# A graph layer on one core: message steps of six and five groups, and three gather groups fetched row by row from another queue

## The reference, cut to what matters

```python
xn = layernorm(x)
# graph layer: mean over the incoming edges of a node, then two linear maps
summed = segment_sum(xn[src], dst, N)
agg = summed / max(counts, 1)
gnn = relu(agg @ W_l.T + b_l + xn @ W_r.T) + xn
# linear attention over all nodes, then an MLP ("message")
Q, K = elu(xn @ Wq) + 1, elu(xn @ Wk) + 1
KV = einsum('nshd,nshv->nhdv', K, (xn @ Wv) / N)
msg = layernorm(attention(Q, KV) @ Wm) * g1 + b1
h = relu(concat[xn, msg] @ W1) @ W2
mix = xn + layernorm(h) * g2 + b2
x = x + gnn + mix
# then a feed-forward on the half of the nodes that a learned score picks
x = x + ffn(layernorm(x))
```

## Time and profile before

| | |
|---|---|
| time, median of 3 runs | 2594.31 us (2593.91 to 2596.81) |
| the profiled execution | 2591.4 us, its span 2589.7 us |
| PE, POOL, DVE, ACT busy | 2200.0, 1696.3, 1316.4, 902.0 us |
| mean granted TensorE clock | 0.937 of full speed |
| gathers (L713) | 1563, 949 ns each |

### The profile page before, as it was taken

How to read it: one execution, slowest core, us unless ns; L and a number is a source line. 1 busy time by engine, 2 the same in 40 slices (tenths; PEclk the granted TensorE clock), 3 DMA queues, 4 the chain that set the end, 5 groups by cost and what they waited for, 6 DMA issues and landing times.

```text
span 2589.7 us, 48874 instructions
## 1 busy us (share of the span) xinstructions
PE 2200.0 (85%) x13352; PEld 1826.8 (71%) x13353; DVE 1316.4 (51%) x3156; ACT 902.0 (35%) x1949; POOL 1696.3 (66%) x1817
## 2 busy tenths in 40 slices
PE   1399999997888888888888888888999899589998
PEld 1287777775667667666676666767777678379998
DVE  8644444443444344454444445544555589844444
ACT  8433333331222222222222222222232258444554
POOL 3577777777777777777777777777777511045553
PEclk6699999998998999999999999999999999689999
DMA  9766666664555555555555555555555489711111
GB/s 332 231 194 187 183 185 180 187 179 149 153 162 156 154 154 165 153 162 156 154 154 152 159 159 162 156 154 154 158 169 158 147 258 295 264 34 46 45 43 35
DMA packets 218372, 419.29 MB, mean 162 GB/s; under 512 B 40579, under 2 KB 107141, under 8 KB 218286
## 3 DMA queue, kind: packets, MB, share of 16 engines
q0 software_dynamic: 88352, 243.57, 33.0%
q1 hardware_dynamic: 129118, 173.95, 20.0%
q10 hardware_dynamic: 816, 0.79, 0.1%
HBM read 321.63 MB, written 96.52 MB: 161 GB/s over the span
## 4 chain that ended last, share of the span: by engine, by line
POOL 37%; PE 37%; issue 14%; DVE 5%; DMA 4%; ACT 1%; DVEq 1%; POOLq 0%; SPq 0%; ACTq 0%
POOL gath_raw L713 37%; PE ps L1779 11%; PE ps L1626 4%; PE ps L1547 3%; PE ps L1719 3%; PE ps L1549 3%; PE ps L1592 3%; DMA gath_raw<-xtab,srcI 3%; PE ps L1636 2%; PE ps L1532 2%; DVE stats L791 1%; PE ps L1674 1%; PE ps L1644 1%; DVE gath_raw L810 1%; PE ps L1715 1%
## 5 line engine op out<-in xcount | busy, mean ns | idle before, releaser
L713 POOL DMA_INDIRECT gath_raw<-xtab,srcI x1563 | 1484.0, 949 | 476.5 <-issue 464.0
L1547 PE MATMUL ps<-gath_raw,onehot 128*128 128x256 f16 x1956 | 477.4, 282 | 205.0 <-DMA gath_raw<-xtab,srcI 115.5
L887 DVE SCALAR_TENSOR_TENSOR onehot<-ps,blkbase,dstF 128x512 f32 x489 | 354.0, 745 | 255.3 <-issue 170.8
L1549 PE MATMUL ps<-gath_raw,onehot 128*128 128x257 f16 x1956 | 478.4, 282 | 0.0
L1547 PEld LDWEIGHTS ps<-gath_raw,onehot 128*128 x1956 | 194.7, 100 | 290.3 <-issue 260.6
L1626 PE MATMUL ps<-work,w_s 128*128 128x256 f32 x1568 | 394.6, 408 | 2.5 <-issue 1.7
L1626 PEld LDWEIGHTS ps<-work,w_s 128*128 128x128 f32 x1568 | 312.5, 205 | 49.8 <-issue 2.7
L961 DVE BATCH_NORM_STATS2 stats<-ps 128x6 f32<-128x256 f32 x196 | 74.4, 422 | 456.7 <-PE ps L1674 452.1
L1779 PE MATMUL ps<-split_raw 128*128 128x256 f32 x2376 | 293.0, 285 | 1.7 <-DVE split_raw L1226 1.5
L1779 PEld LDWEIGHTS ps<-split_raw 128*128 128x128 f32 x2376 | 288.1, 193 | 2.4 <-issue 1.9
L1360 ACT ACTIVATE work<-ps 128x512 f32<-128x512 f32 x98 | 58.5, 597 | 499.5 <-PE ps L1626 499.5
(11 more groups left out here) (215 smaller groups left out, 2990.5 us busy)
## 6 DMA issues: line engine op xcount, KB each, us to landing
work<-x_in SPq DMA_DIRECT2D x98, 256.0 KB
lin_raw<-lin_d POOLq DMA_DIRECT2D x49, 512.0 KB, 4.6
gath_raw<-xtab,srcI POOLq DMA_INDIRECT x1563
agg<-x_in SPq DMA_DIRECT2D x14, 896.0 KB, 7.9
xt_d<-work SPq DMA_DIRECT2D x49, 256.0 KB, 4.3
q_d<-work SPq DMA_DIRECT2D x49, 256.0 KB, 2.5
work<-q_d SPq DMA_DIRECT2D x49, 256.0 KB, 3.3
work<-xt_d SPq DMA_DIRECT2D x49, 256.0 KB, 3.1
```

The source lines that it names most:

```text
L713: e.indirect_dma_start(out=gath[:, TPG * s + t, 0:2 * D], out_offset=None, in_=xtab[:, :], in_offset=bass.IndirectOffsetOnAxis(ap=srcI[:, ...
L887: v.scalar_tensor_tensor(out=onehots[:, ds(p % OHN * TPG, TPG), :], in0=ps[:, columns:columns + 1, 0:P].to_broadcast(shape), scalar=blkbas ...
L1547: t.matmul(ps[:, ds(BG + k % 2, 1), 0:D], oh, gath[:, r, 0:D], start=False, stop=False, skip_group_check=True)
L1549: last = t.matmul(ps[:, ds(BG + k % 2, 1), 0:AGW], oh, gath[:, r, D:2 * D + 1], start=False, stop=q == TPG - 1, skip_group_check=True)
```

## The change

- **Steps.** The message steps take six and five groups in turn (`MPAIR`), 270 in all. 24 groups come behind the steps instead of seven. All steps are now in the loop; only the first two and the last are written out.
- **Place in the ring.** Two steps take eleven groups and the ring has six places, so a group's place changes from one pass of the loop to the next. PE computes it, `(m_first(s, j) + t) % RING`, and each matmul of a message step's `seg` takes the address of its rows from a register. Five semaphores are added (`rows_m`), so that the waits stay fixed to a position among the eleven. The groups behind the steps have constant places again.
- **Three groups row by row.** Groups 371 to 373 (`ROWG`) are not gathered by POOL. SP copies their 1536 rows of 1 KB with one DMA each, 32 in each of 48 message steps, into a buffer of their own (`rowt`). It loads 64 source numbers at a time (`row_list`) into the front of `bnd`, and takes 16 at a time into registers. The buffer has room for eight tiles beside `srcI`; the last four tiles go into the part of `srcI` whose groups are done, for which SP waits once, and then a column of ones is copied in.
- **Room.** The scratch for dynamic DMAs is halved, to 8192 bytes.
- **The end of the sums.** DVE adds the last two blocks' sums with one `add_before` ahead of the wait for the last group and one plain addition behind it, instead of two `add_before` behind it.
- Some semaphores are merged (`edges_set`, `bnd_moved`, `x_rows_in`, `s_placed`); DVE's key-step loop is one pass shorter, with three steps more written out.

```diff
-KG, MG = 2, 6
-NG = NSUP * (KG + MG)
+KG = 2
+MPAIR = (6, 5)
+NG = NSUP * 8
 RING = 6
-TAIL = 7
-MFULL = NSUP - TAIL
+MAT = KG * NSUP
+TAILAT = MAT + sum(MPAIR[i % 2] for i in range(NSUP))
+TAIL = NG - TAILAT
+ROWG = range(TAILAT + 3, TAILAT + 6)
+ROWT = len(ROWG) * TPG
+ROWB = 16
+ROWFREE = 8
...
+            def row_list(tile, half):
+
+                o = ROWG[0] * GE + tile * P + half * 4 * ROWB
+                of = src[o:o + 4 * ROWB] if isinstance(o, int) else src[ds(o, 4 * ROWB)]
+                e.dma_start(row_i, of.rearrange("(o e) -> o e", o=1)).then_inc(row_idx, 16)
+
+            def row_part(tile, half, part):
+
+                _, v = nc.values_load_multi_w_load_instructions(
+                    row_i[:, part * ROWB:(part + 1) * ROWB], engines=[mybir.EngineType.SP], min_val=0, max_val=NPAD - 1,
+                    skip_runtime_bounds_check_because="node numbers below the count of nodes")
+                for k in range(ROWB):
+                    p = half * 4 * ROWB + part * ROWB + k
+                    to = rowt[p:p + 1, ds(tile, 1) if not isinstance(tile, int) else slice(tile, tile + 1), 0:2 * D]
+                    e.dma_start(to.rearrange("p o c -> p (o c)"), xtab[ds(v[k], 1), :]).then_inc(by_row, 16)
+
+            def m_io(i, s, j, tile=None, half=0):
+                if tile is not None and s == 0:
+                    row_list(tile, half)
                 if not (isinstance(i, int) and i == NSUP - 1):
                     if past(i, 1):
                         e.wait_ge(m_xs, i)
                         e.wait_ge(m_nd_ps, i)
                     m_load(i + 1, 1 - s)
+                if tile is not None:
+                    if s == 0:
+                        e.wait_ge(row_idx, 16 * j + 16)
+                        alone(e, stood)
+                    row_part(tile, half, 2 * s)
                 if past(i, 2):
                     e.wait_ge(m_r, i - 1)
                     e.dma_start(turned(r_d, i - 2), flat(mr[s])).then_inc(r_out[s], 16)
...
                     m_load_xT(i + 1, 1 - s)
+                if tile is not None:
+                    row_part(tile, half, 2 * s + 1)
                 if past(i, 2):
                     l_store(i - 2, s)
...
             for g in range(NG):
+                if not fetched(g):
+                    continue
                 s = g % RING
...
-            def seg(slot, use, first, more, end):
-
-                padded = max(0, (use * RING + slot + 1) * TPG - (NG * TPG - GPAD)) if isinstance(use, int) else 0
-                landed = 16 * TPG * use + 16 * (TPG - min(TPG, padded))
+            def seg(rows_of, lists, slot, first, more, end, held=gath):
+
+                row = slot * TPG if isinstance(slot, int) else e.snap(slot * TPG)
+                landed_at = 16 * lists
                 with e.Fori(more, end + 1):
                     p, k = e.snap(pair), e.snap(full)
-                    e.wait_ge(rows_in[slot], landed)
+                    e.wait_ge(rows_of, landed_at)
...
                     for q in range(TPG):
                         oh = onehot[:, ds(p % OHN, 1), q, :]
-                        r = TPG * slot + q
-                        t.matmul(ps[:, ds(BG + k % 2, 1), 0:D], oh, gath[:, r, 0:D], start=False, stop=False,
+                        r = row + q if isinstance(row, int) else ds(row + q, 1)
+                        t.matmul(ps[:, ds(BG + k % 2, 1), 0:D], oh, held[:, r, 0:D], start=False, stop=False,
                                  skip_group_check=True)
-                        last = t.matmul(ps[:, ds(BG + k % 2, 1), 0:AGW], oh, gath[:, r, D:2 * D + 1], start=False,
+                        last = t.matmul(ps[:, ds(BG + k % 2, 1), 0:AGW], oh, held[:, r, D:2 * D + 1], start=False,
                                         stop=q == TPG - 1, skip_group_check=True)
...
+            def m_seg(s, j, t, span):
+
+                g = m_first(s, 0) + t
+                seg(landing(g), landed(g) + TPG * j, (m_first(s, j) + t) % RING, *span)
...
-            e.wait_ge(grp_used, NG)
-            add_before()
-            e.reg_mov(before, held)
-            e.reg_mov(since, pair)
-            add_before()
-            k = e.snap(full)
-            e.wait_ge(seg_added, k + 2)
+            add_before()
+            e.wait_ge(grp_used, NG)
+            b, k = e.snap(held), e.snap(full)
+            v.tensor_tensor(agg[:, ds(b, 1), :], agg[:, ds(b, 1), :], ps[:, ds(BG + k % 2, 1), 0:AGW], ALU.add).then_inc(sum_read, 1)
+            e.wait_ge(sum_read, k + 1)
...
-    nc = bacc.Bacc("TRN2", target_bir_lowering=False, num_devices=1)
+    nc = bacc.Bacc("TRN2", target_bir_lowering=False, num_devices=1, dynamic_dma_scratch_size=8192)
```

More of the change, by code:

```diff
@@ L276, in build @@
         rows_in = [sem(f"rows_in{i}") for i in range(RING)]
-        ones_set = sem("ones_set")
+        rows_m = [sem(f"rows_m{i}") for i in range(sum(MPAIR) - RING)]
+        row_idx = sem("row_idx")
+        by_row = sem("by_row")
         iota_ps = sem("iota_ps")
@@ L281, in build @@
         bnd_tab = sem("bnd_tab")
-        k_x_in = [sem(f"k_x_in{i}") for i in range(3)]
+        x_rows_in = [sem(f"x_rows_in{i}") for i in range(3)]
         k_xn = sem("k_xn")
@@ L299, in build @@
         kvbd_set = sem("kvbd_set")
-        m_x_in = [sem(f"m_x_in{i}") for i in range(2)]
         m_xT_in = [sem(f"m_xT_in{i}") for i in range(2)]
@@ L471, in seg_values, with m_first, fetched, landing @@
             return [tuple(v[3 * t:3 * t + 3]) for t in range(n)]
-        def k_place(s, j, t):
-            return KG * s + t, j
-        def m_first(i):
-            return KG * NSUP + MG * i - (max(0, i - MFULL) if isinstance(i, int) else 0)
-        def m_groups(i):
-            return MG - 1 if isinstance(i, int) and i >= MFULL else MG
-        def place(g):
-            return g % RING, g // RING
-        def m_place(i, t):
-            if isinstance(i, int):
-                return place(m_first(i) + t)
-            slot, use = place(KG * NSUP + t)
-            return slot, use + i
-        tail = list(range(NG - TAIL, NG))
+        def m_first(s, j):
+            return MAT + sum(MPAIR) * j + sum(MPAIR[:s])
+        def fetched(g):
+            return g not in ROWG
+        def landing(g):
+            p = (g - MAT) % sum(MPAIR)
+            return rows_m[p - RING] if MAT <= g < TAILAT and p >= RING else rows_in[g % RING]
+        def landed(g):
+            return TPG * len([o for o in range(g + 1) if landing(o) is landing(g) and fetched(o)])
         key_loads = [(wq_s[:, :, :], Wq.rearrange("(k p) n -> p k n", p=P)),
@@ L618, in m_io @@
                     m_load_xT(i + 1, 1 - s)
+                if tile is not None:
+                    row_part(tile, half, 2 * s + 1)
                 if past(i, 2):
                     l_store(i - 2, s)
-            steps(e, m_io, NSUP, 2)
+            e.wait_ge(grp_used, 2 * ROWB)
+            for s in range(2):
+                m_io(s, s, 0, 0, 0)
+            for tiles, half in ((range(ROWFREE), 0), (range(ROWFREE), 1), (range(ROWFREE, ROWT), 0), (range(ROWFREE, ROWT), 1)):
+                at = half * len(tiles) + 2 * ROWFREE * (tiles[0] // ROWFREE) - tiles[0]
+                if tiles[0] and not half:
+                    e.wait_ge(grp_used, (ROWT - ROWFREE) * RW // 2 // TPG + 1)
+                    with nc.allow_non_contiguous_dma("a column of ones"):
+                        e.dma_start(rowt[:, :, 2 * D:2 * D + 1], gath[:, 0:ROWT, 2 * D:2 * D + 1]).then_inc(by_row, 16)
+                with e.Fori(at + tiles[0] + (1 if at + tiles[0] == 0 else 0), at + tiles[-1] + 1) as j:
+                    for s in range(2):
+                        m_io(j * 2 + s, s, j, j - at, half)
+            m_io(NSUP - 1, (NSUP - 1) % 2, NSUP // 2)
             e.wait_ge(m_r, NSUP - 1)
@@ L1032, in m_body @@
                     l_even(i - 1, 1 - s, j - 1 + s)
-                for t in range(5, m_groups(i)):
+                for t in range(5, MPAIR[s]):
                     seg(g0 + t, BA, *spans[t])
-            steps(e, m_body, MFULL, 2)
-            for i in range(MFULL, NSUP):
-                m_body(i, i % 2, i // 2)
+            steps(e, m_body, NSUP, 2)
             last_two = [(i, own_m + 10 * NSUP - 10 + 5 * k) for k, i in enumerate((NSUP - 2, NSUP - 1))]
-            for t, g in enumerate(tail):
-                seg(g, BA, *seg_values(e, mybir.EngineType.DVE, g, 1)[0])
+            for t in range(RING):
+                seg(TAILAT + t, BA, *seg_values(e, mybir.EngineType.DVE, TAILAT + t, 1)[0])
                 if t in (0, 5):
@@ L1555, in seg @@
                 e.reg_alu(full, behind, 0, op=ALU.max)
[L1556 removed]
+                one = gath[:, 0, 2 * D:2 * D + 1]
                 k = e.snap(full)
@@ L1700, in _ @@
                     m_mlp_out(i)
+            with e.Fori(1, TAIL // RING - 1) as j:
+                spans = seg_values(e, mybir.EngineType.PE, TAILAT + RING * j, RING)
+                for k in range(RING):
```

(5 more changed lines are left out.)

118 lines of the change are left out of this document (60 added, 58 removed).

## The result

The changed kernel takes 2724.4 us (2721.5 to 2726.6) where the kernel before takes 2594.65: a ratio of 1.0502, 95% interval 1.0489 to 1.0514. It is slower by 5%; 2581 us was predicted.

A forecast was written before the change was run, and what follows sets the result against it. It took POOL's gathers to bound the kernel, with PE following. Gains of 15.0, 9.0 and 2.1 us (26.1) less 13 for register places gave -13.1 and 2581 us; the range was 2565 to 2618, the likeliest case 2572 to 2589.

The forecast's parts named there:

- The bound before: Message steps before the change: POOL's gathers set the time from 95 to 2054 us, 5.02 us a group; PE follows.
- Three groups less for POOL: POOL's gathers: 12 fewer at 1.254 us each, -15.0 us, if POOL still never waits.
- The tail: From the last gather's start to the last group's use: 9.3 us instead of 18.35, -9.0.
- DVE's end: The last additions of the sums: one addition and a wait stay of 2.68 us, -2.1.
- SP's rows at 0.5 us: SP's queue in the message steps: 32 rows take 16 us, fitting into its waits; cost 0, bound +60.
- Rival 3: SP's queue becomes the bound at 0.75 us a row or more: steps over 30 us, 2600 to 2650; chance 0.04.
- rest: Merged semaphores, DVE's three key steps written out, and a ones' column copied once: cost 0.
- The register places: PE's row addresses: eight more register instructions a pair at 0.10 us; after the ring POOL stops 12 us, rounded to +13.
- such a block: A block of 16 matmuls on PE, said to hide the register work of the first pair behind it.
- the last two stretches: Late message steps, at 1.37 and 1.41 pairs a group: PE's step forecast at 28.6 and 29.1 us.
- Rival 2: PE becomes the bound at 0.14 us a register instruction: +25 us, 2619, slower than before; chance 0.25.
- Scratch: Dynamic DMA scratch halved: three gathers under way are unaffected; cost 0, doubled waits +3.8 us.

The follow-up runs named there:

- e9b_static_no_rows: Changed kernel without SP's row DMAs, PE waiting for its own groups, PE's message steps written out twelve at a time with constant places: 2580.9 us.
- e10b: Changed kernel with SP's row destinations constant, PE waiting for its own groups, and PE's places constant: 2569.6 us, ratio 0.9893.
- e7: Changed kernel with SP's row destinations constant and PE waiting for its own groups, PE's places still in a register: 2640.4 us.
- e6: Changed kernel without SP's row DMAs (POOL gathers all groups) and with PE waiting for its own groups, places still in a register: 2632.4 us.
- e1_no_rows: Changed kernel without SP's row DMAs, POOL gathering all groups again, the rest kept: 2685.7 us, ratio 1.0332.
- e11: Changed kernel with PE's places constant and PE waiting for its own groups, SP's row destinations still in a register: 2740.0 us.
- e5: Changed kernel with only the semaphore choice altered, so that PE waits for its own groups: 2715.9 us, ratio 1.0464.
- e14b: e9b_static_no_rows with the place of the rows taken from a run-time counter in a register, steps still written out: 2644.5 us, ratio 1.0202.
- e8: e6 with the dynamic DMA scratch at its full size: 2632.45 us.

## Why the prediction was wrong, by its own steps

**The bound before.** Right: in e9b_static_no_rows and e10b POOL sets the pace again, and with PE's need above 27.6 us a step no gather that is taken away buys anything (e7 against e6).

**Three groups less for POOL, -15.0.** Measured -11.3 where POOL is the bound (e10b against e9b); in the profiled executions the last use comes 15.2 us earlier (2051.39 against 2066.61), and 3.1 us are lost in the stages behind, whose length varies between 512 and 518 us from one execution to another, so the term was right. Where PE or SP sets the steps it is worth next to nothing, which the prediction did not say: from the start of the last step to the last gather the changed kernel takes 118.1 us, and e1_no_rows with all gathers 120.2.

**The tail, -9.0, and DVE's end, -2.1.** Right, the first too small. From the last gather to the last use 6.27 us pass (2200.77 to 2207.04) where 18.35 did and 9.3 were predicted; from there to the sums 1.33 us in place of 3.73.

**SP's rows at 0.5 us, cost 0. This is the step that failed.** "With two addresses I take 0.5 us for a row (bounds 0.27 ... and 0.7 ...)": it takes 0.74, above the upper bound, so 32 rows are 23.7 us in place of 16, and SP is full. The bounds came from DMAs with a constant destination, and the added price was put on the address arithmetic. That is not where it lies: the register instruction and the move take 64 and 29 ns, the DMA itself 529 in place of 240, in one and the same kernel. Of 1536 rows 64 have a constant destination. The other 1472 account for (266626 - 222497)/1472 = 30 more DMA packets each than in e10b, and (89155 - 43524)/1472 = 31 more of under 512 B. The sizes of the packets in the trace say what they are: the changed kernel has 23,552 packets of 64 B, 16 for each of the 1472 rows, and e10b has none; in place of one packet of 1024 B a row there are 16 of 64 B and 15 more of 4 B. So a row of 1 KB with its destination in a register goes out in sixteen pieces. The Trainium skill (DMA: Bandwidth & Descriptors, section Why a DMA increments its semaphore by 16 and not by 1) says that software can split one contiguous run into a multiple of 16 so that the engines share it; the packets agree. SP's step became 31.1 us. From the start of the first step to that of the last the changed kernel takes 1485.2 us and e10b 1325.3, which is 159.9 us more; 3.7 come back by the last use, and the spans differ by 156.9 (2724.9 against 2568.0).

Rival 3 was the right mechanism with a chance of 0.04, and the measured 0.74 all but reached its threshold ("0.75 us a row or more"). Its time, 2600 to 2650, was too low, for a step of over 30 us was never multiplied out: 48 steps of 30.5 in place of 27.6 are 139 us more, less the 26 of gain, over 2700. Alone the rows cost 170 us (e11 against e10b); in the changed kernel taking them away bought 39, since two other costs stood behind them.

**The choice of semaphore, not priced.** The prediction's "rest" names merged semaphores at 0, and the text ahead of it says that the waits stay fixed to a position among the eleven; for PE's waits that is so, for the first six groups that POOL counts it is not. The new choice of a group's semaphore makes PE wait for up to the fifth group later: 38 us alone, 53 beside the register places, 8.5 behind SP's rows. Nothing of it can be read from the trace of before; it is in the diff, by writing down for pairs 1 to 5 which group completes the count that is waited for.

**The register places, +13.** The count was right: a pair has 17 register instructions in place of 9. The price of a step was too small: 47 to 71 us in all. "So a first pair behind such a block is free. Not free are the second pair of a group": the first half holds, the second does not. Behind other work both pairs are free, and the cost falls on the first two groups of a step, those behind the table loads, with every pair (about 0.9 us for one, 1.9 for two), where 0.45 each was counted, and on the sixth group. The load's price was misread as well: 1.34 us is the median over two kinds of load, and within the steps of the kernel before the short one takes 0.78 us and the long one 3.9. The step's own need was taken from the earlier trace rows, a stretch at a granted clock of 1.00; the longer gaps come with 0.96. Predicted 28.6 and 29.1 us a step for the last two stretches, measured 29.8 and 30.5 (e6, from 1481 to 1779 and to 1963 us). Rival 2 said 2619 for this alone, the three groups less included; e7, which holds just that, measured 2640.

**Scratch, 0.** Right, within the noise (e8 against e6).

**Left open.** e11 is 24 us slower than e5, although PE has less to do in it; its SP step is 31.7 us in place of 31.1, of which its two blocks of 16 rows account for most (12.03 us each at the median in place of 11.84), and nothing shows why. Nor is it shown why e7 and e14b are 8 and 12 us slower than e6.

## What to carry to other kernels

Here a small DMA with its destination in a register cost the queue twice what the same one with a constant did (529 against 228 ns): price it from a row that has the register, and if the trace has none, do not let a constant one set the upper bound. A semaphore that is picked by a number's residue on one side and by a constant on the other must be checked for every residue: nothing fails when the wait is for something later, only the time is gone. And a control in which a register was meant to be used is worth what its instruction count says: two of these held constants, and "no difference" was an empty answer.

## What the hardware showed beyond what was expected

The load of a step's table of block numbers into registers is long, and its time has no single value. In e6_own_sem_no_rows, by line:

```profile
L476 PEldq TENSOR_LOAD <-bnd x156: 762/1376/5327, 111.0 to 2096.0; - x156
...
L476 DVEq TENSOR_LOAD <-bnd x108: 742/1600/5520, 108.0 to 2087.6; - x108
```

These medians mix loads of different length. Within the message steps PE's load for one group (3 numbers) takes 0.76 to 0.80 us, its load for the others (12 or 15 numbers) 0.86 to 4.13 with a median of 3.0, and DVE's for all groups at once (15 or 18 numbers) 1.55 to 5.48 with a median of 3.4. In the kernel before the medians of the two long ones are 3.9 and 3.7, so DVE's loads are not longer than PE's by much. What sets the time within these bounds is not shown. DVE makes no one-hot of the step until its load is done; whether that costs here was not measured by itself.

And SP's row with a constant destination, at 0.41 us with its address, is a dear way to fetch a row (128 of them are 53 us of SP, against 1.254 us of POOL for a gather), but SP's queue was idle and POOL's set the time: in e10b it brought 11 us.
